# VectorE transposes the attention outputs straight from their bank, and ScalarE no longer copies them in the loop

## The reference

```python
B, S, D, H = 8, 1024, 256, 16          # head width 16, fp32
# attention block
n = layernorm(x)
q, k, v = n @ w_q.T, n @ w_k.T, n @ w_v.T      # split into 16 heads
weights = softmax(einsum('bqhd,bkhd->bhqk', q, k) * 16 ** -0.5)
y = einsum('bhqk,bkhd->bqhd', weights, v).reshape(B, S, D) @ w_o.T
x = x + layernorm(y)
# gated feed-forward block, with a shift by one token
n = layernorm(x)
n_prev = n shifted by one token
xr, xk = mu_r * n + (1 - mu_r) * n_prev, mu_k * n + (1 - mu_k) * n_prev
x = x + layernorm(sigmoid(xr @ W_r.T) * (square(relu(xk @ W_k.T)) @ W_v.T))
```

## Time and profile before

| | before |
|---|---|
| median of 3 runs | 1214.42 us (1211.47 to 1215.19) |
| profiled execution | 1209.24 us |
| its span, first to last instruction | 1207.1 us |
| granted TensorE clock | 1.0 |
| busy: PE / ACT / DVE / POOL | 98% / 87% / 65% / 23% |

### The profile page before, as it was taken

One profiled execution on the slowest core, in us unless ns is written; L12 is line 12 of the kernel. 1 busy time (PEld: TensorE's weight loads), 2 busy tenths in 40 slices (PEclk: granted clock), 3 DMA queues, 4 the chain that ended last, 5 costly groups with the idle time before them and its releaser, 6 DMA issues.

```text
span 1207.1 us, 25766 instructions
## 1 busy us (share of the span) xinstructions
PE 1185.9 (98%) x10588; PEld 652.0 (54%) x10588; DVE 781.3 (65%) x1833; ACT 1055.6 (87%) x1409; POOL 274.3 (23%) x350
## 2 busy tenths in 40 slices
PE   7999999999999999999999999999999999999997
PEld 5544555455555555555555555555555555535455
DVE  7553757758575766847667585766768466464646
ACT  4789898899989999898998989899898999999882
POOL 2000223222221322222222222223222122222132
PEclk9999999999999999999999999999999999999999
DMA  4457563317622185214934166321871139400100
GB/s 162 116 127 192 116 131 79 115 53 140 113 66 89 55 176 105 62 63 113 152 71 123 39 135 117 81 89 54 152 130 47 43 98 160 97 1 19 53 14 23
DMA packets 61943, 113.77 MB, mean 94 GB/s; under 512 B 6528, under 2 KB 31360, under 8 KB 61632
## 3 DMA queue, kind: packets, MB, share of 16 engines
q1 hardware_dynamic: 61504, 110.65, 40.7%
q10 hardware_dynamic: 288, 1.05, 0.3%
HBM read 69.47 MB, written 41.94 MB: 92 GB/s over the span
## 4 chain that ended last, share of the span: by engine, by line
PE 95%; ACT 2%; DVE 2%; DMA 1%; issue 0%; POOL 0%; POOLq 0%; SPq 0%; DVEq 0%
PE O L542 39%; PE M L524 28%; PE M L481 23%; PE M L423 3%; ACT PT L721 1%; PE M L451 1%; PE M L652 1%; DMA xA<-x_dram 1%; DVE sth L926 0%; PE M L645 0%; PE M L629 0%; DVE QS L889 0%; ACT QS L749 0%; PE M L587 0%; DVE xB L1066 0%
## 5 line engine op out<-in xcount | busy, mean ns | idle before, releaser
L721 ACT ACTIVATE PT<-M 128x1024 f32<-128x1024 f32 x1274 | 1000.7, 866 | 110.6 <-PE M L524 99.9
L524 PE MATMUL M<-QS,KS 50*128 50x512 f32 x2048 | 499.9, 419 | 7.9 <-ACT PT L721 7.9
L542 PE MATMUL O<-PT,V 128*17 128x512 f32 x4096 | 490.3, 595 | 0.0
L524 PEld LDWEIGHTS M<-QS,KS 50*128 50x128 f32 x2048 | 221.9, 185 | 264.0 <-ACT PT L721 234.7
L542 PEld LDWEIGHTS O<-PT,V 128*17 128x17 f32 x4096 | 93.3, 96 | 228.6 <-issue 209.5
L481 PE MATMUL M<-xnT,WH 64*128 64x512 f32 x496 | 143.2, 406 | 0.0
L1332 POOL TENSOR_SCALAR veh<-mvh 128x2 f32<-128x2 f32 x90 | 19.9, 221 | 399.6 <-DVE mvh L929 399.6
L1173 DVE SCALAR_TENSOR_TENSOR A<-Z,M 128x512 f32<-128x512 f32 x30 | 20.6, 687 | 110.5 <-PE M L481 110.5
L481 PE MATMUL M<-WH,xnT 64*128 64x256 f32 x480 | 84.6, 284 | 0.0
L481 PE MATMUL M<-WH,C 64*128 64x256 f32 x480 | 84.0, 285 | 0.0
L481 PE MATMUL M<-WH,B 64*128 64x256 f32 x480 | 83.9, 285 | 0.0
(11 more groups left out here) (164 smaller groups left out, 1698.1 us busy)
## 6 DMA issues: line engine op xcount, KB each, us to landing
scr<-p SPq DMA_DIRECT2D x124, 256.0 KB
QS<-scr SPq DMA_DIRECT2D x56, 256.0 KB, 6.8
KS<-scr SPq DMA_DIRECT2D x56, 256.0 KB, 9.5
QS<-scr SPq DMA_DIRECT2D x70, 128.0 KB, 5.6
KS<-scr SPq DMA_DIRECT2D x68, 128.0 KB, 7.8
xA<-x_dram SPq DMA_DIRECT2D x16, 512.0 KB, 7.0
xB<-x_dram SPq DMA_DIRECT2D x16, 512.0 KB, 7.6
out_dram<-xB SPq DMA_DIRECT2D x15, 512.0 KB, 3.2
```

The costliest lines, as they stand in the source:

```text
L524: e.matmul(PM[bank[i, j]], KS[qd][rows, pair, kt * 128:kt * 128 + 128], QS[qd][rows, pair, hf * 512:hf * 512 + 512], start=True, stop=True) \
L542: ins = e.matmul(PO[32 * j:32 * j + 17, :], V[b % 2][:, kt, 4 * qd + j, :], PT[i % 3][:, j, :], start=(kt == 0), stop=(kt == 7))
L721: e.activation(PT[i % 3][:, j:k + 1, :], PB[:, at:at + len(numbers), :], ACT.Exp, scale=SCALE) \
```

## The change

ScalarE's `outputs` is gone. The group's later work gets a stage 0, put first into the list of step 8g+8. In it VectorE turns the outputs straight from the PSUM bank O into `T`, and its end is now what frees O. The division stays in stage 1, where it was. `On` is left to the T pieces and to the last group, so some waits go too.

```diff
@@ plan
         for stage, j in enumerate(quad_at(g)):
             rests[j].append((("quad", g), stage + 1))
+        rests[8 * g + 8].insert(0, (("quad", g), 0))
@@ scalar
-            def outputs(g):
-                p.wait_ge(("values", 8 * g + 7), ("On_turned", g - 1) if g else ("warm", 5))
-                for word, n in filter(None, TURNS[8 * g:8 * g + 8]):
-                    if word in ("T00", "T10"):
-                        p.wait_ge(("xnT", n, 0, int(word[1])))
-                e.activation(On[:, :], PO[:, :], ACT.Copy).then_inc(*up(act_wrote, ("PO", g)))
...
-                    p.wait_ge(("values", 8 * g + 7), ("On_turned", g - 1))
+                    p.wait_ge(("values", 8 * g + 7), ("xnT", B - 1, 0, 1))
...
-                if i % 8 == 7:
-                    outputs(i // 8)
...
-                if i % 8 == 0:
-                    outputs(i // 8 - 1)
@@ vector, after_T
-                    p.wait_ge(("piece", piece), ("On_turned", (turned_at(piece) - 1) // 8 - 1))
+                    p.wait_ge(("piece", piece))
@@ vector, after_quad
-                if stage == 1:
-                    p.wait_ge(("PO", g), ("T_read", g - 2) if g >= 2 else ("parted", "wr"))
-                    e.transpose(at[:, :], On[:, :]).then_inc(*note(("On_turned", g)))
-                    p.wait_ge(("On_turned", g))
+                if stage == 0:
+                    p.wait_ge(("values", 8 * g + 7), ("T_read", g - 2) if g >= 2 else ("parted", "wr"))
+                    e.transpose(at[:, :], PO[:, :]).then_inc(*note(("PO", g)))
+                elif stage == 1:
+                    p.wait_ge(("PO", g))
                     e.reciprocal(rec[:, :], view[:, :, 16]).then_inc(*note(("rec", g)))
```

More of the change, by code:

```diff
@@ L955, in after_T @@
                     lower(xnT[1][:, c, cols], On[:, :], xnT[0][:, c, cols].bitcast(F32), ("hi", piece), ("xnT", b, c, g))
-            def turned_at(piece):
-                return TURNS.index(piece)
             def after_QK(piece, stage, head=False):
```

## The result

The changed kernel takes 1247.7 us (median of 4 runs, 1246.12 to 1248.81). The kernel before, with one more run beside it, takes 1213.87 us (median of 4, 1211.47 to 1215.19). The ratio on record is 1.0294, 95% interval 1.0271 to 1.0317 (the two medians as they stand give 1.028): 3% slower, as forecast, 5 us under the forecast of 1253 and inside its range. The span of the profiled execution is 1245.9 us against 1207.1.

A forecast was written before the change was run, and what follows sets the result against it. TensorE's own queue, tied to ScalarE by scores and exponentials, was taken as the bound. 16.0 + 12.4 + 9.4 + 2.65 - 1.4 - 0.7 = +38.3 us gave 1252.7 from the median, stated as 1253 us, range 1240 to 1263.

The forecast's parts named there:

- The bound: TensorE's own queue, tied to ScalarE by one round of scores and exponentials, sets a period of 4.4 us.
- the idle 0.56 us: ScalarE's idle time in a period with the copy of O, taken to show that ScalarE has room.
- ScalarE is the real bound: Rival: a good part of ScalarE's 38.1 us of copies comes back, 1176 to 1186 us; chance 0.04.
- The gain: Without ScalarE's copy, 0.03 us back at about 48 of 62 places, -1.4 us; last unit -0.7 us.
- The last unit: VectorE's transpose for O moves into an idle stretch, off the chain to z's turns: -0.7 us.
- The transpose from the bank: VectorE's transpose of O from PSUM takes 0.70 us, upper bound 0.95; from SBUF 691 ns.
- Slot 8: Units 1 to 14: transpose stands behind y0's stage 1, values matmuls start 1.14 us late; 16.0 us in all.
- Slot 16: Transpose delays z1's mixes and a bank wanted at slot 18: 2.07 us 6 times, 1.34 us 7 times.
- Step 8: Once: weights, a norm and K11's emptying precede the transpose in VectorE's queue; load 2.65 us late.
- Slots 0 and 24: VectorE long idle there, O free over 1.5 us before it is wanted; cost nothing.
- From the profile to the median: Adds the 5.2 us by which the profiled execution lay under the median: 1247.6 us becomes 1252.7.
- The rivals: Hidden bank wait at slot 18 0.08, not slower 0.05, ScalarE the real bound 0.04, costs more 0.08.

The follow-up runs named there:

- run 6: kernel 4 plus two unused ScalarE copies of a weight into `On` per group, where the old copy stood: 1244.5 us, ratio 1.0278.
- kernel 4: Changed kernel with O's transpose ahead of y0's stage 1, between z1's two stages, and the very first at step 7: 1212.13 us, ratio 1.0003.
- run 5: kernel 4 plus one unused ScalarE copy of a weight into `On` per group, where the old copy stood: 1212.08 us, ratio 1.0002.
- kernel 1: Changed kernel with only the slot 8 transpose of O moved ahead of y0's stage 1, units 1 to 14: 1237.45 us, ratio 1.022.
- kernel 2: Changed kernel with only the slot 16 transpose of O moved between z1's stages 1 and 2: 1228.97 us, ratio 1.0163.
- kernel 3: Changed kernel with the slot 8 transpose of O moved ahead of y0's stage 1 in unit 14 alone: 1247.21 us, measured once.
- kernel 11: kernel 4, but with the very first transpose of O late, as in the changed kernel: 1213.2 us, ratio 1.0015.

## Why the prediction was right, and where it was off

**The bound.** Right. The period moved by some 0.03 us and the wait for exponentials by 2 us in 235 when ScalarE lost its copies, neither moved when it got as much back, and both did when it got as much once more. One step towards it was wrong: the idle 0.56 us of the earlier trace rows were read as room, and run 6 shows that they are none. The forecast of 38 us less busy time was wrong too, 27.0: it took the copies' own lengths and no overlap. *ScalarE is the real bound* is refuted by kernel 4 and run 5.

**The gain.** -0.01 to -0.07 us in each period that had the copy, -1.5 us in all, for -1.4. The last unit gave 0.56 us where z is turned, for 0.7, and 0.37 at slot 26, which was not in the sum and is ScalarE's copy (run 5).

**The transpose from the bank.** I took 0.70 us, with 0.95 as bound. It takes 709 ns against 691 from SBUF:

```profile
L986 DVE STREAM_TRANSPOSE T<-O 128x512 f32<-128x512 f32 x63 | 44.7, 709 | 54.0 <-PE O L543 54.0
```

These 18 ns are, as an estimate, +0.5 us over the 27 stalls (14 + 6 + 7). So this operation does care where its source is, by 18 ns, which the two subtractions of the earlier trace rows (691 and 692 ns) did not show.

**Slot 8.** 1.11 to 1.15 us for 1.14. The argument (the aggregate ends, the transpose runs, the load follows) is what the four rows above show, one after the other. That it is the place and not the operation is shown by kernel 1.

**Slot 16.** The mechanism was right, in both kinds of unit, and is shown by kernel 2. The size was off by 8%: 1.90 for 2.07 and 1.22 for 1.34. The load itself came as late as forecast. It started 365.05 - 362.87 = 2.18 us after the burst of slot 16 before and 379.29 - 375.04 = 4.25 us after it now, 2.07 us later in unit 4; in unit 5 1.35 us later, for 1.34. But a later load is not a later period to the same amount: from the load to the next burst unit 4 takes 2.07 us now and took 2.20. Why is not shown; that TensorE had a little of the other rows' work done during the wait is likely.

**Step 8.** 2.65 us, as worked out.

**Slots 0 and 24.** "Cost nothing" is what was measured, and for unit 1 it was luck. Kernel 4, without the delay of step 8, waits 2.0 us for the transpose at slot 0 of unit 1. The step that VectorE has long been idle there fails at this place: it has two emptyings into `p` ahead of the transpose, and they wait for a transfer.

**From the profile to the median.** This step failed. I added the 5.2 us by which the profiled execution lay under the median, as if they were the same in both kernels. They were not: in the second profile of the kernel before they are a wait (1.74 us) and a lower clock (0.77 of 110 to 125 us) in unit 1, and the changed kernel did not show that in either of its profiles. It showed other losses of clock instead, 3.1 us in the first. The median of three runs was also a high one, for a cause that is open: beside the experiments the kernel before had medians of 1210.24, 1210.56 and 1210.57 us in sets of 7, 23 and 13 runs, only 1.0 to 1.3 us over the profiled 1209.24. The sum on the profiled execution, 1209.24 + 38.3 = 1247.6 us, met the median of 1247.7 with two errors that cancel, which is luck: terms 2.4 us too large (38.3 for 35.9), and lower clock that I had not in the sum (3.1).

**The chances.** The rivals add up to 0.25 (0.08, 0.05, 0.04, 0.08), not to the 0.2 that the text beside the range says.

**Not foreseen at all:** a lower clock behind a stall. It was 3 us here, and 8 to 9 us in the two profiles of kernel 1, which had fewer stalls.

## What to carry to other kernels

The single accumulation bank was free when the engine that reads it got to it in its own order, so the moved read had two prices: what stands ahead of it in the new queue (the bank's next user waits, 1.11 to 1.15 us at slot 8), and what is ready behind it while it waits for the bank (slot 16: 1.43 us of VectorE idle in unit 4, and 1.83 to 1.94 us at slot 18 of the even units). Both are read from the neighbours in the queue before anything is run, and at these places both were cured by a place in a gap of that queue, not by a faster read. A neighbour that waits for a transfer belongs to them too: at slot 0 of unit 1 it cost nothing in the changed kernel, and 2.0 us of wait in kernel 4, where the engines come there earlier. Relieving an engine pays only if a period gets shorter without its work (here by 0.01 to 0.07 us, for 38.1 us of copies); put the same work there again, unused, and once more, and the price of it is measured.

## What the runs showed of the hardware that I had not expected

- Stalls of TensorE of 1.1 to 2.6 us were in some places followed by a stretch with a granted clock of 0.50. Outside the last 5 us of each span there are 22 such stretches in the 13 profiles: 20 of 3.4 us, and 2 of 6.8 us, in unit 1 of kernel 5 and of the kernel before (its second profile). Behind the stall of step 8 the granted clock of 61.0 to 64.5 us was 0.51 to 0.70 in the 6 profiles of kernels 1, 2, 3 and the changed one, and 1.00 in kernel 11. Most stalls are not followed by it: of some 28 of 0.9 us and more in each profile of the changed kernel 2 were, in those of kernel 1 it was 6 of 15 and 5 of 14, in kernel 2 1 of 15, in kernel 3 1 of 28.
- Where a drop comes varies between executions of one kernel: unit 14 once and unit 10 once in the changed kernel. And one drop had no such stall before it: in kernel 6 the clock fell at slot 12 of unit 14 (0.51 in the 3.5 us from 1086.8) behind a wait of 0.41 us.
- At 110 to 125 us, at the start of unit 1, 4 of the 6 profiles without the stall of step 8 showed a lower clock (0.77 and 0.89 in the windows), and none of the 7 with it. In all four TensorE had just stood idle, 1.7 us in the kernel before, 2.0 twice in kernel 4 and 2.5 in kernel 5, each time behind VectorE's emptying into `p` and the transfer `scr<-p`. Where it idled less at this place, 1.3 us in kernel 6 and 0.3 in kernel 11, the clock was 1.00. So these drops too come behind a stall. Why the emptying is later in one execution of the kernel before than in the other, and why kernel 1 lost more clock behind slot 18 than the changed kernel did, stays open.
- A block transpose of 128x512 in fp32 on VectorE took 18 ns more from PSUM in the changed kernel than from SBUF in the kernel before (709 against 691 ns, 63 each).
